# Copies of products, context and output projection in the last four steps: VectorE in place of ScalarE

## The reference

```python
# attention, per batch: 8 heads of 16 channels, query = key = value
q = xt @ Wq.T                                   # xt: 256 x 128
scores = scale * einsum('bhqd,bhkd->bhqk', qh, qh)
logits = (scores * cmask + (1.0 - cmask) * NEG) * rmask
ctx = einsum('bhqk,bhkd->bhqd', softmax(logits), qh)
h = transpose(ctx @ Wo.T)                       # 16 x 128 x 256
# experts: each of the 16 * 128 rows of 256 is one token
logits = einsum('th,eh->te', x, router_w)       # 8 experts
top_vals, top_idx = top_k(logits, 2)
weight = softmax(top_vals)[:, 0]
out = x_in + weight * expert[top_idx[:, 0]](x)  # silu(gate) * up, then down
```

## Time and profile before

| what | value |
|---|---|
| median of 3 timed runs | 236.3 us (236.2 to 237.83) |
| profiled execution: span from first to last instruction | 250.4 us |
| mean granted TensorE clock in it | 0.962 |
| PE, PEld busy | 222.5 us (89%), 152.6 us (61%) |
| DVE, ACT, POOL busy | 146.8 us (59%), 131.8 us (53%), 114.0 us (46%) |
| steps 16 to 19 in the span | about 142 to 163 us |

### The profile page before, as it was taken

The page is one execution under the profiler, slowest core; times in us unless marked ns, Lnnn a source line. Parts: engine busy times, 40 slices in busy tenths (PEclk is TensorE's granted clock), DMA queues, the critical chain, the costliest instruction groups (busy, mean ns, idle before and its releaser), DMA issues.

```text
span 250.4 us, 5450 instructions
## 1 busy us (share of the span) xinstructions
PE 222.5 (89%) x1739; PEld 152.6 (61%) x1739; DVE 146.8 (59%) x403; ACT 131.8 (53%) x298; POOL 114.0 (46%) x211
## 2 busy tenths in 40 slices
PE   7989999999999999999999998879954899949960
PEld 6988566665666576656666654647722576727740
DVE  3787957877987888788878767438300132312330
ACT  2431677777777877768778788254211233312410
POOL 4855645643652564255001130441775254744451
PEclk9999999999999999999999999999997599997995
DMA  6785767987769675676542300270455034242110
GB/s 170 179 196 125 202 167 203 277 214 209 210 176 274 172 189 157 161 216 162 133 115 60 103 24 27 73 228 22 127 151 166 9 100 134 72 146 66 43 36 0
DMA packets 44731, 34.39 MB, mean 137 GB/s; under 512 B 5708, under 2 KB 42719, under 8 KB 44704
## 3 DMA queue, kind: packets, MB, share of 16 engines
q1 hardware_dynamic: 26896, 18.77, 27.8%
q0 software_dynamic: 2944, 8.24, 11.3%
q10 hardware_dynamic: 14864, 7.04, 11.0%
HBM read 16.91 MB, written 7.28 MB: 97 GB/s over the span
## 4 chain that ended last, share of the span: by engine, by line
PE 67%; ACT 8%; DMA 5%; issue 5%; SPq 3%; DVE 3%; another core or an unknown queue 3%; ACTq 2%; POOL 1%; POOLq 0%; DVEq 0%
PE bank L714 12%; PE bank L591 10%; PE bank L567 9%; PE bank L579 9%; ACT probs L798 6%; PE bank L733 4%; PE bank L735 4%; PE bank L620 4%; PE bank L532 3%; SPq L431 3%; PE bank L725 2%; PE bank L547 2%; PE bank L705 2%; PE bank L612 2%
## 5 line engine op out<-in xcount | busy, mean ns | idle before, releaser
L930 DVE TENSOR_REDUCE row_max<-bank 128x2 f32<-128x512 f32 x128 | 85.0, 687 | 24.0 <-PE bank L567 23.8
L798 ACT ACTIVATE probs<-bank 128x512 f32<-128x512 f32 x128 | 76.2, 600 | 25.3 <-PE bank L579 22.5
L567 PE MATMUL bank<-stack 96*128 96x256 bf16 x256 | 49.5, 274 | 1.5 <-DMA stack<-parts 1.4
L579 PE MATMUL bank<-stack 99*128 99x256 bf16 x256 | 49.0, 272 | 0.9 <-ACT probs L798 0.5
L391 POOL DMA_INDIRECT out<-y_sb,put_i x23 | 23.1, 1006 | 31.8 <-DVE y_sb L1196 28.2
L591 PE MATMUL bank<-probs,v_sb 128*32 128x256 f32 x512 | 34.3, 385 | 0.2 <-ACT probs L798 0.2
L714 PE MATMUL bank<-gu_sb,gotT 128*128 x92 | 33.8, 492 | 0.0
L567 PEld LDWEIGHTS bank<-stack 96*128 96x128 bf16 x256 | 21.0, 98 | 19.5 <-DVE row_max L930 10.7
L1188 DVE SCALAR_TENSOR_TENSOR act_sb<-silu,got,bank 128x176 f32<-128x176 f32 x23 | 9.1, 397 | 39.9 <-ACT silu L879 27.8
L295 POOL TENSOR_TENSOR qm<-q_sb,cond_all 128x256 f32<-128x256 f32 x15 | 11.1, 738 | 44.6 <-ACT q_sb L783 44.6
L381 POOL DMA_INDIRECT got<-rows_dram,take_i x23 | 22.5, 977 | 17.7 <-DVE take_i L1085 9.4
(11 more groups left out here) (153 smaller groups left out, 302.9 us busy)
## 6 DMA issues: line engine op xcount, KB each, us to landing
stack<-parts SPq DMA_DIRECT2D x96, 64.0 KB, 2.6
stack<-parts ACTq DMA_DIRECT2D x96, 64.0 KB, 2.8
gu_sb<-in_guT SPq DMA_DIRECT2D x8, 352.0 KB, 3.9
rows_dram<-h_sb SPq DMA_DIRECT2D x16, 132.5 KB, 2.3
x_sb<-in_x SPq DMA_DIRECT2D x16, 128.0 KB, 3.7
rows_dram<-in_x SPq DMA_DIRECT2D x4, 512.0 KB, 4.9
cond_all<-in_cond SPq DMA_DIRECT2D x12, 128.0 KB, 4.3
dn_sb<-in_dnT SPq DMA_DIRECT2D x4, 256.0 KB, 3.5
```

The costliest lines, as they stand in the source:

```text
L567: mm = t_.matmul(bank[h % 2][:, q * T:(q + 1) * T], stack[k][0:ROWS, 0, h, q * P:(q + 1) * P], stack[k][0:ROWS, 1, h, :], start=True, stop ...
L579: mm = t_.matmul(bank[2 + h % 2][:, q * T:(q + 1) * T], stack[k][0:ROWS2, 0, h, q * P:(q + 1) * P], stack[k][0:ROWS2, 1, h, :], start=True ...
L798: a.activation(probs[:, h, :, :].rearrange("p k t -> p (k t)"), bank[2 + h % 2][:, 0:NT * T], ACT.Exp, scale=float(DK) ** -0.5).then_inc(e ...
L930: v.tensor_reduce(row_max[:, b % 2, :, h:h + 1], bank[h % 2][:, 0:NT * T].rearrange("p (q k) -> p q k", q=NT), AX.X, ALU.max).then_inc(max ...
```

## The change

From step 16 on (`s >= B`) ScalarE no longer makes the three copies; VectorE has them instead, in three new functions: four hidden copies (batches 12 to 15), three of products and three of contexts (batches 13 to 15), ten copies in all. Sizes, buffers and what each waits for stay. In slot 1 of VectorE the products of batch s-3 stand first, then the hidden copy of batch s-4, then `find_top`. The context copy stands in slot 6.

```diff
@@ ScalarE
-                    if h == 0 and there(s - 4):
+                    if h == 0 and there(s - 4) and s < B:
                         copy_hidden(s - 4)
-                    if h == 1 and there(s - 3):
+                    if h == 1 and there(s - 3) and s < B:
                         copy_products(s - 3)
...
-                    if h == 6 and there(s - 3):
+                    if h == 6 and there(s - 3) and s < B:
                         copy_context(s - 3)
@@ VectorE
+            def last_hidden(b):
+                dve.wait_ge(h_done, b + 1)
+                dve.wait_ge(h_out[b % 3], 16 * (b // 3))
+                v.tensor_copy(h_sb[:, b % 3, 0:HL], bank[POST][:, 0:HL]).then_inc(h_copied, 1)
+                dve.wait_ge(h_copied, b + 1)
+
+            def last_products(b):
+                dve.wait_ge(pv_done, NG * (b + 1))
+                dve.wait_ge(pvT_done, b)
+                v.tensor_copy(pv_sb[:, :, :].rearrange("p g t -> p (g t)"), bank[PV][:, :]).then_inc(pv_copied, 1)
+
+            def last_context(b):
+                dve.wait_ge(cx_done, b + 1)
+                dve.wait_ge(h_done, b)
+                v.tensor_copy(cx_sb[:, :], bank[POST][:, 0:HL]).then_inc(cx_copied, 1)
@@ VectorE, the loop
+                    if h == 1 and there(s - 3) and s >= B:
+                        last_products(s - 3)
                     if h == 1 and there(s - 4):
+                        if s >= B:
+                            last_hidden(s - 4)
                         find_top(s - 4)
...
+                    if h == 6 and there(s - 3) and s >= B:
+                        last_context(s - 3)
                     if h == 7 and there(s - 4):
                         make_gate(s - 4)
```

## The result

The change took 245.52 us in the median of its first four runs (244.13 to 246.04), the kernel before 236.25: a ratio of 1.039, 95% interval 1.033 to 1.046, some 9.3 us slower. That is above my range, which ended at 244.6. Two more series of the same kernel beside the kernel before gave ratios of 1.026 (1.020 to 1.033) and 1.034 (1.029 to 1.039). Means and ratios leave out runs over 1.5% above the fastest of the same kernel, two of the change's sixteen and six of the forty-four of the kernel before. Over what is left of the three series the change averages 244.4 us and the kernel before 236.6: 7.8 us. That mean lies just inside my range; the first series lies above it.

A forecast was written before the change was run, and what follows sets the result against it. It took a chain of waits relayed between TensorE, ScalarE's copies and VectorE as the bound, with overlaps needing two engines. From 236.3 us, steps 16 to 18 added +1.6, +0.6, +1.5 and +1.3, giving 241.3; range 238.3 to 244.6.

The forecast's parts named there:

- Price of a copy: VectorE's copies out of PSUM: 0.62 us for the products to the next start, 0.43 for the small ones; lower end 0.27.
- Step 16, start: VectorE copies products and hidden rows before `find_top(12)`, so `rank_early` and TensorE's queue behind it come 1.6 us later.
- Step 16, end: VectorE copies the context of batch 13 only after `early_places`, delaying `project_out(13)`: +0.6 us, together +2.2.
- Step 17: `find_top(13)` waits behind products and hidden rows, moving `normalize(14)` and what follows: +1.5 us, together +3.7.
- Step 18: `find_top(14)` waits for `apply_probs(15, 1)` and copies: +1.3 us, together +5.0 at `keep_warm`; first gather 5.3 later.
- The sum: Whole kernel: 236.3 + 1.6 + 0.6 + 1.5 + 1.3 = 241.3 us.
- the first rival: TensorE's clock falls in the new gaps between 144 and 166 us: some 4 us, 245 in all; chance 0.10.
- The expert stage: After the attention's tail: it hangs on the delayed chain and adds 0 us, so +5.0 carries to the end.
- Slack at the gathers: Expert stage's gathers absorb the delays of steps 17 and 18; only step 16 counts: +2.2 us, 238.5; chance 0.12.
- ScalarE as the bound: Steps 16 and 17 give back 2 us of ScalarE's copies: 234.3, at the very most 231.9; chance 0.06.

## Why the prediction was wrong, point by point

- **Price of a copy: right.** Taken 0.62 and 0.43, measured 0.61 to the next start and 0.42 (0.53 to the next start). The lower end of 0.27 for a small copy is shut out: f32 from PSUM did not go as fast as the bf16 copy. The Trainium skill, "VectorE: DVE Perf Modes", sections on the errata and on the perf-mode tiers, gives a f32 copy out of PSUM 120 cycles and one more for each element. The estimates made from it, 0.40 and 0.66 us, agree within 5% with the 0.42 and 0.69 us measured.
- **Step 16, start: right.** `rank_early` +1.55 in the change, +1.54 with the clock held, forecast 1.6. The run with `rank_early` moved and the one with the memset show the wait itself.
- **Step 16, end: right where the clock holds.** TensorE waits 0.63 us for the context in that profile, forecast 0.6. In the profile with the fall this wait is covered by TensorE's own lateness.
- **Step 17: right in its mechanism, 0.2 low.** At full clock `normalize(14)` comes 157.31 - 144.18 = 13.13 us after `apply_probs(13, 1)` begins (second profile of the change, VectorE), before 152.30 - 143.10 = 9.20: +3.9, forecast +3.7. The search-to-`normalize` distance stayed at 1.97 us.
- **Step 18: right.** Gather +5.5 with the clock held, forecast +5.3; `keep_warm` +5.2 (167.67 - 144.18 = 23.49, before 161.44 - 143.10 = 18.34), forecast +5.0.
- **The step that failed is the clock.** The sum of 241.3 has no term for TensorE's clock in steps 16 and 17; its fall was the first rival, with a chance of 0.10, because "the new gaps have whole bursts of 1 to 2 us between them". Two of three profiles show it, in both places, and it puts the gather 2.0 to 2.2 us later. The chance was too low and the price of some 4 us too high. Against the bursts stood a fact in my own rows: the clock had fallen in the expert stage after TensorE was busy 0.45 of 2 us, and my own sums left TensorE two waits in step 17 between 152.85, the end of `apply_probs(14, 1)`, and `turn_context(14)` behind 156.0. I did not put the two side by side. It would not have made the fall certain: the change fell after stretches of 0.71 and 0.45 of 2 us, and held its clock in another profile after 0.62 and 0.44; the kernel before held it after 0.17 of 2 us (166 to 168 us, second profile). No row here says when it falls.
- **The expert stage: 0, within its scatter.** From the first gather to the end the spans leave 75.7 us in the second profile of before, 75.1, 75.7 and 74.8 in the three of the change, and 74.0 to 76.6 in the other runs; only the odd first profile of before has 91.3.
- **The sum.** The 7.8 us in the mean of all series are 5.5 of queue (the sum carried 5.0), some 1.4 of clock (two of three profiles at 2.0 to 2.2, an estimate), and 0.9 that I can't place. The first series, with 9.3 us, had four low clocks of four (0.976 to 0.978): 5.5 and 2.2, and 1.6 not placed. So of the 4.2 us by which 245.5 misses 241.3, about 2.2 are the clock, 0.5 the queue, and the rest is not placed. The medians of the first and third series (245.52 and 244.94) lie above the range and that of the second (244.23) within it; on which side a series falls is in part the luck of the clock. With the gaps filled the median lies 6.5 to 6.7 us above before, where the distance says 5.5. The profiles show where that microsecond is: in both the clock falls behind the gathers, to 0.50 within the stretch from 172 to 176 us, gate and up take 1.72 and 2.50 us (1.96 and 2.26 in the second) where the second profile of the change has 1.35 twice, and 76.6 us are left from the first gather to the end. So the filled gaps held the clock in steps 16 and 17 and lost about 1 us of the gain in the expert stage. The runs with a memset are 0.8 to 2.0 above their distances; what makes that, and the 0.9, stays open. The start of step 16 alone varies by 3.6 us from profile to profile.
- **The other rivals.** Slack at the gathers: none found, the delays of `rank_early` made with a memset (1.42 and 0.57 us) arrived at the gather whole (1.43 and 0.58), and the change's grew from +1.5 in step 16 to +3.9 and +5.5. ScalarE as the bound: not seen, hidden copies alone on VectorE give a ratio of 0.999, with the search 0.6 us earlier and the gather no earlier.

## What to carry to other kernels

- Moving work to the engine with more idle time can cost little by its length and much by its place: ask what the moved instruction waits for, and what then stands behind that wait. Here ten copies cost 5.5 us on the path in one order (7.7 with the clock's fall) and 1.3 in another.
- On an in-order engine, put what is ready first. The products' copy could not start before `apply_probs` ended; the search could.
- A gap that a change opens on TensorE can be priced twice, once by its length and once by the clock after it. Where new gaps open and the same trace shows the clock fall elsewhere, take both outcomes into the range, with and without the fall. Here the same kernel had both, 2.0 to 2.2 us apart.
- One profile shows one outcome. The single series of four runs had only low clocks, and the second profile the other level.

## What was not expected of the hardware

- The fall of the clock is not tied to the program alone: with gaps equal to 0.01 us the same kernel kept 1.00 in one profile and fell to 0.50 in two. The same gaps of step 17 (0.70 and 1.63 us) left the clock at full in the profile in which step 16's gap was split in two.
- With a gap of 1.26 us alone two of four runs had a mean clock of 0.975 and 0.980; with one of 0.41 us none of twelve was below 0.982, and none of the 72 runs of the kernel before was below 0.980. Where in the two runs the clock fell is not shown.
- A f32 matmul of 128 by 128 columns makes two records of 0.11 us, 0.22 in all. A filling sized with 0.11 us for each matmul is twice too long.
